# A planned two-block transformer kernel: normalizations in halves, one-pass turning of the remainder, and two head-start items moved behind the first maxima

## The chip, the cores and the metric

One Trainium2 chip, and of it one core. The core has five engines with a queue each: TensorE (PE in the profile; its weight loads are PEld), VectorE (DVE), ScalarE (ACT), GpSimd (POOL) and SyncE (SP, which here only issues DMAs). The metric is the device time of one execution in microseconds (us).

## The reference

Two transformer blocks run one after the other on x of 2 batches x 512 tokens x 144 columns, in float32, with 16 heads of 9 columns. Each block is modulated by six vectors from a condition. The second block's attention is causal, and its MLP uses SiLU where the first has GELU.

```python
ada = silu(c) @ W_ada + b_ada
shift_msa, scale_msa, gate_msa, shift_mlp, scale_mlp, gate_mlp = split(ada, 6)
h = layernorm(x) * (1 + scale_msa) + shift_msa
x = x + gate_msa * attention(h)            # softmax(q k^T / 3) v, then @ W_proj + b_proj
h = layernorm(x) * (1 + scale_mlp) + shift_mlp
x = x + gate_mlp * (gelu(h @ W_fc1 + b_fc1) @ W_fc2 + b_fc2)
# block 2: the same, causal mask, silu in the MLP, weights Wq, Wk, Wv, Wp, W1, W2
```

## The kernel before

**Tiling.** 512 tokens are 4 tiles of 128. The 144 columns are 128 columns and a remainder of 16. A normalization (l, b, k) belongs to block l, batch b, and attention (k 0) or MLP (k 1). It consists of items: `stats` (VectorE: mean and variance of each tile, L1191 to L1196; then GpSimd: `rstd`, L911), `norm` (VectorE: hn, L1204), `hr` (the remainder is modulated and split into a high and a low part in hs, five instructions, L715 to L719, on GpSimd or VectorE), and two `hT` items (TensorE turns hn or hs with four matmuls against an identity, L1350; ScalarE copies the result to hT or hT_s, L1007 and L1003). The last number of such an item is its part: 0 is all four tiles, 1 and 2 are halves. Before the change only the very last normalization runs in halves.

**Attention.** The heads are handled in 16 groups of 4: groups 0 to 3 are block 1, batch 1; 4 to 7 block 1, batch 2; 8 to 11 and 12 to 15 the same for block 2. For each group g there are 16 `max` items (TensorE: queries x keys, L1396; VectorE: the maximum of each row, L1247, or L1244 with the mask in block 2), `msplit` (GpSimd: four small instructions, L967 to L970), `mT` (TensorE turns the maxima, L1406; ScalarE copies, L1043; GpSimd sends them by DMA into rows of QS, L978), 16 `scores` items (TensorE, L1417; ScalarE: exp into probs, L1053), four `pv` items (TensorE: probs x V, four matmuls each, L1437), and `o` (ScalarE copies OT, L1060; TensorE turns it, L1444; VectorE divides, L1259 and L1260). I write M2:5 for the sixth max item of group 2 and S2:5 for the scores. `qk` makes queries and keys, `mid` and `low` split them in three bf16 parts, which go to DRAM (SP, L758) and come back as rows of QS and KS (SP, L771), `v` the values; `aT` and `proj` the output projection, `fc1`, `tanh`, `gate`, `fc2` and `fc2b` the MLP. `agate`, `acol` and GpSimd's `gated`, `fcs` and `stackw` prepare weights.

**The array.** Max and scores matmuls use half of the array's rows; two that follow each other on opposite halves run at once. pv uses quarters of its columns, everything else the whole array.

**What sets the order.** `steps` lists every item with an assumed cost, the items that it waits for, and for some a time before which it is not placed (the table `loaded`). `plan` then runs a list schedule in Python, when the program is built: on each engine it takes the item of the highest urgency (longest chain behind it, plus an offset from the table HASTE) among those that can start soon. SLACK says how soon, HOLD and OTHERS how many of the seven PSUM banks a stream may hold (three for max and three for scores). Where the plan expects TensorE to wait and its load to be low, it puts in `FILL` matmuls, identity times identity, whose result nobody reads (L1305). The plan's order is fixed in the program: on the chip each engine works strictly in that order and waits on semaphores. So a late item delays everything behind it on its engine. A program that prints the order lists what stands on each engine.

## Time and profile before

| | before |
|---|---|
| median of 3 runs | 301.45 us (299.92 to 302.79) |
| profiled execution, device time | 298.9 us |
| its span in the trace | 297.2 us |
| TensorE busy | 278.5 us, 94% |
| VectorE busy | 223.8 us, 75% |
| ScalarE busy | 185.5 us, 62% |
| GpSimd busy | 111.0 us, 37% |
| granted TensorE clock, mean | 0.994 |

The profiled execution is 2.6 us under the median of the three timed ones; 1.7 us of it lie outside the span. The page gives busy times and the costliest groups of instructions, the trace gives each instruction with its start and what ended the idle time before it. A TensorE matmul of float32 shows as two records. Durations of matmuls are modelled from issue to drained result, so neighbours overlap; how long TensorE is held is read from one start to the next.

### The profile page before, as it was taken

The numbers are of one execution on the slowest core, as the hardware profiler recorded it, in microseconds if no ns is written. First come the engines' busy times: TensorE is split into PE (matmuls) and PEld (weight loads), VectorE is DVE, ScalarE is ACT, GpSimd is POOL, SyncE is SP. The second block draws the span as 40 slices with busy tenths as digits, with TensorE's granted clock in tenths as the row PEclk, the third lists the DMA queues.
The fourth block names the chain that finished last, engine by engine and source line by source line (L and its number), as shares of the span: only waits on it lengthen the run. The fifth ranks groups of instructions, "written<-read, shape, count | busy, mean of one in ns | idle before, by whom it ended". The sixth has DMA issues, their size and how long they took to land.

```text
span 297.2 us, 5866 instructions
## 1 busy us (share of the span) xinstructions
PE 278.5 (94%) x1855; PEld 139.6 (47%) x1855; DVE 223.8 (75%) x674; ACT 185.5 (62%) x405; POOL 111.0 (37%) x242
## 2 busy tenths in 40 slices
PE   5999899999999999999998799999998999999996
PEld 4946444243243544543333434943422444344975
DVE  6859999999799986866465687498996997514761
ACT  2242326788876679667786469175756786895160
POOL 6104855936515232051331350144354455640100
PEclk9999999999999999999999999999997999999999
DMA  7514575452000000000045200000353000000001
GB/s 219 125 16 126 163 192 164 145 159 91 3 2 2 5 0 2 2 0 0 5 123 157 82 1 0 4 1 5 92 166 106 2 3 4 2 2 1 21 22 40
DMA packets 19038, 16.75 MB, mean 56 GB/s; under 512 B 2410, under 2 KB 18477, under 8 KB 19008
## 3 DMA queue, kind: packets, MB, share of 16 engines
q1 hardware_dynamic: 17214, 15.63, 18.2%
q10 hardware_dynamic: 706, 0.55, 0.6%
q0 software_dynamic: 1088, 0.20, 0.4%
q8 instruction: 15, 0.25, 0.3%
q14 instruction: 15, 0.12, 0.1%
HBM read 9.34 MB, written 6.34 MB: 53 GB/s over the span
## 4 chain that ended last, share of the span: by engine, by line
PE 68%; DVE 10%; issue 8%; ACT 8%; DMA 4%; POOL 3%; ACTq 0%; POOLq 0%
PE OB L1437 13%; PE PB L1417 9%; PE PB L1396 8%; PE PB L1471 6%; PE PB L1487 5%; ACT probs L1053 4%; PE PB L1305 4%; DVE top L1247 3%; PE PB L1444 3%; PE PB L1360 3%; PE PB L1350 2%; DMA QS<-mT 2%; PE PB L1338 2%; PE PB L1463 2%; PE PB L1472 2%
## 5 line engine op out<-in xcount | busy, mean ns | idle before, releaser
L1053 ACT ACTIVATE probs<-PB 128x512 f32<-128x512 f32 (+3 forms) x256 | 113.6, 523 | 44.6 <-PE PB L1417 32.2
L1247 DVE TENSOR_REDUCE top<-PB 128x1 f32<-128x512 f32 x128 | 79.7, 680 | 5.8 <-PE PB L1396 5.4
L1244 DVE CUSTOM_DVE_ANT_0 PB<-PB,mask_qk 128x128 f32<-128x128 f32 (+3 forms) x128 | 58.9, 521 | 10.4 <-PE PB L1396 10.3
L1396 PE MATMUL PB<-KS,QS 61*128 61x512 bf16 (+3 forms) x256 | 59.7, 345 | 2.5 <-issue 1.1
L1417 PE MATMUL PB<-QS,KS 64*128 64x512 bf16 (+3 forms) x256 | 58.0, 344 | 2.3 <-DMA QS<-mT 1.7
L1437 PE MATMUL OB<-probs,V 128*10 128x512 f32 (+3 forms) x512 | 57.0, 524 | 0.8 <-POOL probs L954 0.6
L1417 PEld LDWEIGHTS PB<-QS,KS 64*128 64x128 bf16 x256 | 16.7, 94 | 35.5 <-issue 22.1
L1396 PEld LDWEIGHTS PB<-KS,QS 61*128 61x128 bf16 x256 | 16.6, 94 | 33.9 <-issue 21.1
L954 POOL TENSOR_SCALAR_AFFINE_SELECT probs<-probs 128x512 f32<-128x512 f32 x32 | 20.3, 636 | 25.9 <-ACT probs L1053 24.9
L978 POOL DMA_DIRECT2D QS<-mT x32 | 18.5, 579 | 28.0 <-ACT mT L1043 27.1
L1305 PE MATMUL PB<-ident 128*128 128x128 f32 x116 | 23.9, 328 | 3.9 <-POOL ident L855 3.4
L1305 PEld LDWEIGHTS PB<-ident 128*128 128x128 f32 x116 | 18.1, 216 | 11.2 <-issue 5.3
L1471 PE MATMUL PB<-hT,w_fc 128*128 128x512 f32 (+3 forms) x50 | 22.0, 526 | 0.1
L911 POOL TENSOR_TENSOR rstd<-veps,half 128x4 f32<-128x4 f32 (+1 forms) x9 | 8.7, 968 | 30.2 <-DVE veps L1196 30.2
L903 POOL TENSOR_TENSOR parts<-rest,parts 108x512 bf16<-108x512 f32 x8 | 9.2, 1154 | 25.3 <-ACT parts L1025 25.3
L1437 PEld LDWEIGHTS OB<-probs,V 128*10 128x10 f32 x512 | 8.1, 89 | 20.8 <-issue 12.9
L1244 DVE DVE_READ_ACCUMULATOR2_ANT top<- 128x1 f32 x128 | 17.8, 139 | 0.0
L1268 DVE TENSOR_TENSOR X<-X,PB 128x288 f32<-128x288 f32 x16 | 7.2, 451 | 14.0 <-PE PB L1487 10.2
L1007 ACT ACTIVATE hT<-PB,mod 128x512 f32<-128x512 f32 (+1 forms) x9 | 6.7, 743 | 16.0 <-PE PB L1350 16.0
L1487 PE MATMUL PB<-g_fc,U 128*128 128x144 f32 (+1 forms) x120 | 15.7, 286 | 0.0
L1487 PEld LDWEIGHTS PB<-g_fc,U 128*128 128x128 f32 (+1 forms) x120 | 15.0, 190 | 0.9 <-ACT probs L1053 0.9
L1472 PE MATMUL PB<-hT_s,w_fc_s 96*128 96x512 f32 (+3 forms) x25 | 15.3, 612 | 0.0
(155 smaller groups left out, 404.3 us busy)
## 6 DMA issues: line engine op xcount, KB each, us to landing
qk_parts<-parts SPq DMA_DIRECT2D x16, 162.0 KB
QS<-qk_parts SPq DMA_DIRECT2D x16, 162.0 KB
KS<-qk_parts SPq DMA_DIRECT2D x16, 162.0 KB
qk_parts<-parts SPq DMA_DIRECT2D x18, 108.0 KB
qk_parts<-parts SPq DMA_DIRECT2D x16, 54.0 KB
w_fc<-in_L_cond_W_fc SPq DMA_DIRECT2D x2, 288.0 KB
w_fc<-in_L_cond_W SPq DMA_DIRECT2D x2, 288.0 KB
out<-X SPq DMA_DIRECT2D x4, 144.0 KB, 1.9
```

Of the source, the lines that this page charges most:

```text
L954: nc.gpsimd.affine_select(out=p, in_=p, compare_op=ALU.is_ge, fill=0.0, base=0, pattern=[[0, HG], [1, P]], channel_multiplier=-1).then_inc ...
L978: pool.dma_start(QS[b][STRIP * q + SROW:STRIP * (q + 1), h // 2:h // 2 + 2, :], mT[6 * q:6 * q + 6, g % 2, :]).then_inc(m_in[g % 2], 16)
L1053: nc.scalar.activation(probs[:, kt % 2, j, q0:T], bank_of(item)[:, q0:T], ACT.Exp, scale=SCALE).then_inc(bank_free[BANK[item]], 1)
L1244: ins = nc.vector.tensor_tensor_reduce(bank[:, 0:w], bank[:, 0:w], mask_qk[:, T - w:T], 1.0, NEG, ALU.add, ALU.max, m)
L1247: ins = nc.vector.tensor_reduce(m, bank[:, 0:w], AX.X, ALU.max)
L1305: nc.tensor.matmul(bank[:, 0:P], ident[:, :], ident[:, :], start=True, stop=True)
L1396: ins = nc.tensor.matmul(bank[:, 0:w], QS[b][rows, i, qt * P:(qt + 1) * P], KS[b][rows, i, 0:w], start=True, stop=True)
L1417: ins = nc.tensor.matmul(bank[:, q0:T], KS[b][rows, i, kt * P:(kt + 1) * P], QS[b][rows, i, q0:T], start=True, stop=True)
L1437: ins = nc.tensor.matmul(OB[CT * j:CT * j + VW, q0:T], V[b][:, kt, h + j, :], probs[:, kt % 2, j, q0:T], start=(kt == 0), stop=(kt == NT - 1))
L1471: nc.tensor.matmul(bank[0:w, tok], w_fc1[l][:, cols], hT[in_last(l, b)][:, tok], start=True, stop=False)
L1472: nc.tensor.matmul(bank[0:w, tok], w_fc1_s[l][:, cols], hT_s[in_last(l, b)][:, tok], start=False, stop=True).then_inc(filled_bank, 1)
L1487: ins = nc.tensor.matmul(bank[:, t * C:(t + 1) * C], (xh if in_last(l, b) else U)[0:w, c, tok], g_fc2[l][b][0:w, c, :], start=c == 0 and n ...
```

## The change

1. **Halves.** `normed_in` names the normalizations that stay whole (the first of each batch in block 1, and the MLP's of block 2, batch 1). The four others, (0,0,1), (1,0,0), (0,1,1) and (1,1,0) as block, batch, kind, now run in two halves, and the first half of each stands between the two `proj` or the two `fc2` items. qk, v and fc1 wait for both.
2. **The remainder's turning.** The matmuls of `hT` with r = 1 are float32r matmuls against a float32r identity (`identr`, one more VectorE copy at the start), no longer float32 transposes.
3. **The remainder on VectorE.** The second half's `hr` of the four moves from GpSimd to VectorE (`ON_DVE`).
4. **Times in `loaded`.** The second batch's first `stats` may be placed only from 33 us of the plan's time (before: 8), `fcs` of block 1 from 45 (33), `gated` of block 1 from 47 (40).
5. **The planner.** Streams max and scores get a bonus while they hold few banks (`FEED`), the limits of banks and SLACK change, and all of HASTE is new, so that the order changes nearly everywhere. The plan's filler matmuls are 48 (before 58).

```diff
+def normed_in(l, b, k):
+    return (0,) if (l, b, k) in ((0, 0, 0), (0, 1, 0), (L - 1, 0, 1)) else (1, 2)
+def norm_items(l, b, k, n):
+    parts = normed_in(l, b, k)
+    items = [[(kind, l, b, k, s) for kind in ("stats", "norm", "hr")] for s in parts]
+    turned = [("hT", l, b, k, r, s) for s in parts for r in range(2)]
+    if len(parts) == 1:
+        return ([], items[0], turned)[n + 1 if n < 2 else 0] if k == 0 and l == 0 else ([], [], items[0] + turned)[n]
+    return ([], items[0], items[1] + turned)[n]
...
-        return ([("aT", l, b, r, 0) for r in range(2)] + [("proj", l, b, i) for i in range(2)]
-                + [("stats", l, b, 1, 0), ("norm", l, b, 1, 0), ("hr", l, b, 1, 0), ("hT", l, b, 1, 0, 0), ("hT", l, b, 1, 1, 0)]
-                + mlp_items(l, b, 0) + [(kind, l, b, i) for i in range(2) for kind in ("fc2", "fc2b")])
+        return ([("aT", l, b, r, 0) for r in range(2)] + [("proj", l, b, 0)] + norm_items(l, b, 1, 1) + [("proj", l, b, 1)] + norm_items(l, b, 1, 2)
+                + mlp_items(l, b, 0) + [(kind, l, b, 0) for kind in ("fc2", "fc2b")] + (norm_items(l + 1, b, 0, 1) if l == 0 else [])
+                + [(kind, l, b, 1) for kind in ("fc2", "fc2b")])
...
-ON_DVE = [("hr", 0, 0, 0, 0), ("hr", 1, 1, 1, 1), ("hr", 1, 1, 1, 2)]
+ON_DVE = [("hr", 0, 0, 0, 0), ("hr", 0, 0, 1, 2), ("hr", 1, 0, 0, 2), ("hr", 0, 1, 1, 2), ("hr", 1, 1, 0, 2), ("hr", 1, 1, 1, 1), ("hr", 1, 1, 1, 2)]
...
-    loaded = {("acol", 0, 0): 5600, ("stats", 0, 0, 0, 0): 4800, ("wcopy", 0): 6000, ("stats", 0, 1, 0, 0): 8000,
+    loaded = {("acol", 0, 0): 5600, ("stats", 0, 0, 0, 0): 4800, ("wcopy", 0): 6000, ("stats", 0, 1, 0, 0): 33000,
...
-HOLD = {"attend": 3, "max": 3, "shift": 3}
-OTHERS, CALM = 2, 5
+FEED = {"max": (453000, 533000), "attend": (319000, 939000)}
+HOLD = {"attend": 3, "max": 3, "shift": 2}
+OTHERS, CALM = 3, 4
...
-    "gather": (-89000, -1231000, -28000, -333000, -1129000, -586000, -1383000, 3000, 2000, 51000, 391000, 342000, -1000, 0, 240000, 37000),
+    "gather": (-517000, -329000, -20000, -613000, -85000, -415000, -273000, -4000, 0, -126000, -181000, -165000, 311000, 44000, 189000, -75000),
...
-SLACK = {"PE": 100, "ACT": 0, "DVE": 200, "POOL": 100}
+SLACK = {"PE": 100, "ACT": 0, "DVE": 0, "POOL": 500}
...
+            dve.wait_ge(consts, 1)
+            nc.vector.tensor_copy(identr[:, :], ident[:, :])
...
-                        src = hs[:, t, :].bitcast(F32) if r else hn[:, t, 0:P]
-                        n = SR if r else P
-                        ins = nc.tensor.transpose(bank[0:n, t * P:(t + 1) * P], src, ident[:, :])
+                        o = bank[0:SR if r else P, t * P:(t + 1) * P]
+                        ins = (nc.tensor.matmul(o, hs[:, t, :], identr[:, :], start=True, stop=True) if r
+                               else nc.tensor.transpose(o, hn[:, t, 0:P], ident[:, :]))
```

The order on VectorE from the first batch's last qk split on, before. L1191 to L1204 are the second batch's first normalization, L1247 the maxima of groups 0 to 2, L1221 and L1227 the splits of the second batch's queries and keys:

```order
L1191 BN_STATS stat<-X 128x6 x4
L1194 BN_AGGR mean<-stat 128x2 x4
L1196 TENSOR_SCALAR veps<-mean 128x4
L1247 TENSOR_REDUCE top<-PB 128x1 x6
L1204 TENSOR_SCALAR hn<-X,mean,rstd 128x144 x4
L1247 TENSOR_REDUCE top<-PB 128x1 x9
L1221 TENSOR_TENSOR rest<-PB,parts 72x512
L1247 TENSOR_REDUCE top<-PB 128x1
L1227 TENSOR_TENSOR parts<-rest,parts 72x512
L1221 TENSOR_TENSOR rest<-PB,parts 108x512
L1247 TENSOR_REDUCE top<-PB 128x1 x8
```

The same place in the changed kernel, where every line number is 25 higher:

```order
L1272 TENSOR_REDUCE top<-PB 128x1 x16
L1216 BN_STATS stat<-X 128x6 x4
L1219 BN_AGGR mean<-stat 128x2 x4
L1221 TENSOR_SCALAR veps<-mean 128x4
L1229 TENSOR_SCALAR hn<-X,mean,rstd 128x144 x4
L1272 TENSOR_REDUCE top<-PB 128x1 x16
L1246 TENSOR_TENSOR rest<-PB,parts 72x512
L1272 TENSOR_REDUCE top<-PB 128x1
L1252 TENSOR_TENSOR parts<-rest,parts 72x512
L1246 TENSOR_TENSOR rest<-PB,parts 108x512
```

All 16 maxima of group 0 now come first, then the statistics, and directly behind them hn, with no maximum between.

GpSimd at the same place, before, from the second batch's rstd to the DMA of group 0's maxima (L939 to L943, L876 and L878 are `fcs`, the first MLP's weights):

```order
L911 TENSOR_TENSOR rstd<-veps,half 128x4
...
L719 TENSOR_TENSOR hs<-hy,hs 128x4x16
L939 MEMSET w_fc_s 96x576
...
L876 CAST w_fc_s<-raw_f 17x576 x2
L878 TENSOR_TENSOR w_fc_s<-raw_f,w_fc_s 17x576
L967 CAST msp<-top 128x4x2x2
...
L970 TENSOR_TENSOR msp<-mrest,msp 128x4x2x2
L903 TENSOR_TENSOR parts<-rest,parts 108x512
L978 DMA QS<-mT 3x2x512 x2
```

And in the changed kernel (here lines are 23 higher), up to the weights:

```order
L990 CAST msp<-top 128x4x2x2
L991 TENSOR_TENSOR mrest<-top,msp 128x16
L992 CAST msp<-mrest 128x4x2x2
L993 TENSOR_TENSOR msp<-mrest,msp 128x4x2x2
L934 TENSOR_TENSOR rstd<-veps,half 128x4
L1001 DMA QS<-mT 3x2x512 x2
L738 TENSOR_TENSOR hy<-hn,modr 128x64
...
L742 TENSOR_TENSOR hs<-hy,hs 128x4x16
L962 MEMSET w_fc_s 96x576
```

Group 0's maxima are split and sent ahead of the second batch's remainder and of the weights; only its rstd stands between.

On VectorE, behind the second batch's first `proj` in block 1 (L1293, before L1268), the changed kernel has this (L1269 are masked maxima of block 2, two rows each):

```order
L1293 TENSOR_TENSOR X<-X,PB 128x288
L1269 ISA PB,top<-PB,mask_qk 128x128
L1269 ISA top 128x1
L1216 BN_STATS stat<-X 128x6 x2
L1219 BN_AGGR mean<-stat 128x2 x2
L1221 TENSOR_SCALAR veps<-mean 128x2
...
L1229 TENSOR_SCALAR hn<-X,mean,rstd 128x144 x2
L1293 TENSOR_TENSOR X<-X,PB 128x288
L1269 ISA PB,top<-PB,mask_qk 128x256
L1269 ISA top 128x1
L1216 BN_STATS stat<-X 128x6 x2
```

Before, both additions to X came first, then the statistics of four tiles; now the first half's statistics and hn lie ahead of the second addition.

## Rows read from the trace of the kernel before

**Rows 1.** The page: busy time, share of the span, instructions.
```profile
PE 278.5 (94%) x1855; PEld 139.6 (47%) x1855; DVE 223.8 (75%) x674; ACT 185.5 (62%) x405; POOL 111.0 (37%) x242
```

**Rows 2.** Busy time by stretch (windows).
```profile
core 0: us, PE busy (x) PEld busy (x) DVE busy (x) ACT busy (x) POOL busy (x), PEclk, DMA share, GB/s
23.48:45.51 22.03, 20.33 (x103) 11.02 (x102) 21.32 (x44) 6.92 (x13) 12.37 (x22) 1.00 0.59 169
45.51:95.18 49.67, 49.18 (x345) 18.31 (x344) 45.65 (x92) 38.42 (x76) 25.80 (x60) 1.00 0.27 81
149.45:200.84 51.39, 46.41 (x329) 24.37 (x325) 36.64 (x138) 33.07 (x72) 14.15 (x32) 1.00 0.18 53
225.00:230.00 5.00, 4.90 (x31) 1.32 (x34) 3.63 (x21) 2.70 (x8) 2.40 (x4) 0.68 0.30 86
```

**Rows 3.** TensorE in order of time: start us, us, line, op, tiles, shapes, count.
```profile
23.48 0.60 PE L1396 MATMUL PB<-KS,QS 61*128 61x512 bf16 x3
24.01 0.49 PE L1305 MATMUL PB<-ident 128*128 128x128 f32 x2
24.43 0.39 PE L1396 MATMUL PB<-KS,QS 61*128 61x512 bf16 x1
24.75 0.49 PE L1305 MATMUL PB<-ident 128*128 128x128 f32 x2
...
94.62 0.63 PE L1444 MATMUL PB<-ident,OT 128*128 128x128 f32 x4
95.18 0.39 PE L1396 MATMUL PB<-KS,QS 61*128 61x512 bf16 x1
```

**Rows 4.** VectorE in order of time, from the second batch's statistics on.
```profile
24.81 0.69 DVE L1196 TENSOR_SCALAR veps<-mean 128x4 f32<-128x4 f32 x1
25.41 3.67 DVE L1247 TENSOR_REDUCE top<-PB 128x1 f32<-128x512 f32 x6
29.00 1.14 DVE L1204 TENSOR_SCALAR hn<-X,mean,rstd 128x144 f32<-128x144 f32 x4
...
36.20 0.68 DVE L1247 TENSOR_REDUCE top<-PB 128x1 f32<-128x512 f32 x1
```

**Rows 5.** GpSimd: a split beside L1196, and group 0's maxima.
```profile
24.32 1.15 POOL L903 TENSOR_TENSOR parts<-rest,parts 108x512 bf16<-108x512 f32 x1 [1.01 <-ACT parts L1025]
37.14 0.61 POOL L967 CAST msp<-top 128x16 bf16<-128x16 f32 x1
40.52 1.24 POOL L978 DMA_DIRECT2D QS<-mT  x2 [0.29 <-POOL parts L903]
```

**Rows 6.** TensorE: values from the remainder (float32r), then the remainder turned.
```profile
22.40 0.44 PE L1378 MATMUL PB<-w_s,hT_s 96*128 96x144 f32 x2
22.67 0.70 PE L1378 MATMUL PB<-raw,hT 128*128 128x144 f32 x4
...
32.01 0.61 PE L1350 MATMUL PB<-ident,hs 128*96 128x128 f32 x4 [0.62 <-POOL hs L719]
32.55 0.39 PE L1396 MATMUL PB<-KS,QS 61*128 61x512 bf16 x2
```

**Rows 7.** The second batch's MLP normalization in block 1, on VectorE and GpSimd.
```profile
166.55 0.45 DVE L1268 TENSOR_TENSOR X<-X,PB 128x288 f32<-128x288 f32 x1 [0.53 <-PE PB L1463]
167.10 0.94 DVE L1191 BATCH_NORM_STATS2 stat<-X 128x6 f32<-128x144 f32 x4
168.49 0.17 DVE L1196 TENSOR_SCALAR veps<-mean 128x4 f32<-128x4 f32 x1
...
168.75 1.03 POOL L911 TENSOR_TENSOR rstd<-veps,half 128x4 f32<-128x4 f32 x1 [3.94 <-DVE veps L1196]
...
172.71 0.32 POOL L715 TENSOR_TENSOR hy<-hn,modr 128x64 f32<-128x64 f32 x1
...
173.99 0.30 POOL L719 TENSOR_TENSOR hs<-hy,hs 128x64 fp32r<-128x64 f32 x1
```

**Rows 8.** What VectorE waited for over the whole span: us, times, longest (waits).
```profile
DVE hn L1204 <- POOL rstd L911: 3.4, 3, 2.4
```

More of the change, by code:

```diff
@@ L452, in plan @@
                     calm = at["PE", "max"] == 0 or at["PE", "attend"] == len(queues["PE", "attend"])
+                    if group in FEED and sum(mine) < 2:
+                        pressed = FEED[group][sum(mine)]
                     if sum(mine) >= HOLD.get(group, CALM if calm else OTHERS):
@@ L709, in remainder @@
             if earlier:
-                full(eng, ("hT", *earlier[-1], 1, 0))
+                full(eng, ("hT", *earlier[-1], 1, normed_in(*earlier[-1])[-1]))
             else:
```

62 lines of the change are left out of this document (33 added, 29 removed).

## The prediction

> **What bounds the kernel now.** I read the page first: TensorE is busy 94% of the span, VectorE 75%, ScalarE 62% [rows 1]. Shares over the whole span hide where a second engine binds, so next the windows. Between the first max matmul and M6:0 VectorE too is nearly full: 21.32 of 22.03 us, then 45.65 of 49.67 us, beside TensorE's 49.18 [rows 2]. There both are full, and neither can gain alone. From 149 to 201 us, where the second batch passes from block 1 to block 2, TensorE is busy for 46.41 of 51.39 us and VectorE for 36.64 [rows 2]: there both wait for chains. Then the order in time, for what TensorE is held by. Three max matmuls take 0.53 us (two at once, 0.22, the third 0.22, and 0.09 for the turn from half of the array's rows to all); a max followed by such a turn 0.32 us; a filler with a turn on each side 0.42 us, so 0.22 without them [rows 3]. Last, I placed a landmark: the fourth `o` starts at 94.62 us and the matmul of M6:0 at 95.18 us [rows 3].
>
> **Counting both orders.** I counted the TensorE items of both programs up to M6:0 and behind it. Most are the same in both and drop out of a difference. Counted from M0:0 (23.48 us):
>
> - Up to M6:0, before: 68 scores, 16 pv, 4 o, 94 turns, 23 fillers. Changed: 62 scores, 14 pv, 3 o, 80 turns, 14 fillers, 2 fewer pairs at once.
> - Behind M6:0, before: 187 turns, 24 fillers, 145 pairs. Changed: 227 turns, 22 fillers, 162 pairs, and the 6 scores, 2 pv and the o that were not done.
>
> **Step 1, the head, up to M6:0: -3.7 us.** In the changed kernel VectorE sets this stretch. It has 96 maxima, at 0.60 us each (six take the 3.59 us from 25.41 to 29.00 [rows 4]) 57.6 us. To that come, each read from such a row or a neighbour of it, the statistics 1.5, hn 1.1, four splits of queries and keys 2.5, three o 1.5, three agate and two acol 2.2 us. And there is a new wait. Before, six maxima lie between statistics and hn; now nothing does. GpSimd's rstd takes about 1.03 us [rows 7], so VectorE stands for 1.2 us with handovers, unless GpSimd is still at the split of group 0, which needs 1.5 us from 33.5 us on and is done as the statistics end. Sum 67.6 us. VectorE starts the maxima at 23.8 instead of 25.41 us [rows 4], since the statistics are no longer ahead of them, so it is through at 91.4 us. TensorE may be some maxima ahead of it (three banks), which allows 90 us for the matmul of M6:0. Its own work is smaller, 61.7 us by the counts, which alone would allow 85 us. As both interfere at times (before, VectorE stood for some 4 us in this stretch though it was nearly full), I take 91.5 us, against 95.18. Scores start some 5 us earlier, because GpSimd takes up group 0's maxima at about 33.6 instead of 37.14 us and sends them at about 36.8 instead of 40.52 us [rows 5]. But by itself this is worth nothing: the maxima don't run faster.
>
> GpSimd's weights that moved behind cost nothing: it is busy 25.80 of 49.67 us [rows 2], and fc1 and proj need them only after 99 us. The second batch's rows arrive later, by up to 7 us by my reading, and are due at M4:0, at about 69 us; I see about 2 us of cover. If it is gone, each us more is a us lost.
>
> On beside-work the Trainium skill has a rule that speaks against the move. L1196 took 0.69 us while GpSimd's L903 ran from 24.32 to 25.47 us [rows 4, 5], and 0.17 us with GpSimd idle [rows 7]. The page "GPSIMD Engine Reference" (Specifications) says that GpSimd's SBUF ports are shared with VectorE and collide with VectorE instructions of some kinds. By that rule the moved statistics, now beside GpSimd's four instructions on group 0's maxima, could be stretched again, by some 0.5 us; the trace agrees as far as this one row goes. By the row alone the price is 0 to 0.5 us, and it was paid before too, so the sum has nothing for it.
>
> **Step 2, TensorE's content behind M6:0: +4.4 us.** Forty turns more at 0.09 are +3.6 us. Two fillers fewer are -0.4. 17 pairs more, less 6 scores more: -1.0 us by width (block 2's are narrower, down to 128 columns). Two pv and one o that were put off are +2.5 us. The turned remainder: before, four take 0.54 us [rows 6]. A float32r matmul of 144 columns took 0.135 us [rows 6], four would be 0.54 us too, a gain of nothing; its weights have 128 columns where hs has 96, so at best three quarters, 0.40 us. I take 0.5 us less over all of them. (From the row, 0 to 1.1 us.)
> The page "TensorE: Matmul & The Clock Gate" (LDWEIGHTS) gives a weight load columns divided by 1.2 ns, 80 ns for 96 columns. By it four would be 0.32 us and the gain some 1.8 us in all, which is 1.3 us under my sum; no row here has such a load alone.
> Sum: 3.6 - 0.4 - 1.0 + 2.5 - 0.5 = 4.2, and rounding of the tally 0.2.
>
> **Step 3, halves: -4.4 us.** fc1 and qk need both halves, so what counts is the chain from the last addition to X on. It loses half of the statistics (1.32 us, L1191 and L1194: -0.65), half of hn (1.1 us [rows 4]: -0.55), and in place of GpSimd's 1.58 us from 172.71 to 174.29 us [rows 7] VectorE does half a remainder, 0.75 us (-0.8); half of the turning goes too (-0.2). That is 2.2 us. rstd stays: 1.03 us [rows 7] is nearly all fixed cost. Four normalizations are halved, but only where TensorE waits does it count. (0,0,1) and (1,0,0) run while it is full. (0,1,1) and (1,1,0) lie in the stretch with 5 us of idle time [rows 2] and most of the late fillers. 2 x 2.2 = 4.4 us, less than the idle time there. Bounds: 0, if other waits take its place, and -8, if fillers go with it.
>
> **Step 4, not changed.** The order from the last `o` on, some 26 us, is the same but for line numbers. The clock's dip (0.68 of full speed in 5 us, 1.6 us lost [rows 2]) may come or not; I leave it.
>
> **Sum.** Span 297.2 - 3.7 + 4.4 - 4.4 = 293.5 us. 1.7 us outside it: 295.2 against 298.9 us of the profiled execution. That one was 2.6 us under the median of the timed runs, 301.45 us, and I predict their median: **297.8 us**, 1.2% faster.
>
> **The rivals.**
> *A. The halves give nothing (chance 0.31).* TensorE's waits at the second batch's passage are then for the exp chain and the maxima's DMA, not for the norms; the new order has as many fillers there as before (16 against 17), which speaks for it. Then step 3 is 0 to -2: 300 to 302 us, no difference to be told from none. That the halves don't shorten the chain at all, as each needs its own rstd, comes to the same.
> *B. Each half makes VectorE stand for its rstd (0.24), slower.* Now VectorE stood three times, 3.4 us in all, for rstd [rows 8]. In halves there are four waits more, and at (1,0,0) the new order puts hn directly behind the statistics. GpSimd works in order too, and a wait of its own (a causal cut, a DMA that waits for ScalarE) then holds VectorE. At 1.2 us each, with the head's, it is 6 us on VectorE. It decides the time when VectorE's waits for rstd pass some 5 us and fall where the maxima are needed next; with nothing from step 3, the time is 302.2 + 3 = 305 us. Against it: three of the first halves have one to four maxima between.
> *C. TensorE's content alone decides (0.12, of the 0.45 for faster).* If VectorE's idle time in the head is not needed, M6:0 comes at 90 us, and fillers shrink the passage: 293.5 to 295 us.
>
> **How the numbers follow.** My case, 296 to 298.4 us, has 0.33 and is the likeliest, C 0.12, A 0.31, B 0.24. Under 1% nothing can be told from no change by this kernel's measurement; a part of my case's upper end falls there, and a part of A's under it, which cancel. Faster by over 1% (under 298.4 us) 0.45, within 1% 0.31, slower (over 304.5 us) 0.24. The range holds 8 in 10: 292.5 to 305.5 us, from C's lower end to B's price. My own case's range is 294.5 to 301.
>
> **What would show it.** Step 1: M6:0 near 91.5 us, VectorE with one idle time of about 1.2 us before L1229 at 35 us and full otherwise; wrong if M6:0 is later than 94 us, or if TensorE waits at M4:0 for rows of QS and KS. Step 2: the span from M6:0 to the end no shorter than before if step 3 fails. Step 3: from the second proj's addition to the first fc1 matmul at (0,1,1) about 2 us shorter, and TensorE's idle time in the passage down to 1 us or less. Wrong in all: the waits for rstd over 6 us, or another clock dip.

## The result: slower by 3.8%, and the profile after

| | before | changed |
|---|---|---|
| median | 302.12 us (299.92 to 303.82) | 312.87 us (311.59 to 316.12) |
| ratio | | 1.0376, 95% interval 1.027 to 1.0482 |
| span of the profiled execution | 297.2 us | 309.6 us |
| granted TensorE clock, mean | 0.994 | 0.967 |

I had predicted 297.8 us (292.5 to 305.5). The direction was wrong, and the time lies outside the range. Medians are over all timed executions of a kernel; a ratio leaves out those that ran over 1.5% slower than its fastest, so the two can differ a little.

The page's busy times of the changed kernel, to be held against [rows 1]:

```profile
PE 284.2 (92%) x1835; PEld 139.0 (45%) x1835; DVE 229.1 (74%) x699; ACT 187.5 (61%) x413; POOL 112.4 (36%) x246
```

TensorE is busy 5.7 us longer with 20 records fewer, and the span grew by 12.4 us. So part is work and part is standing; a part of the longer work is the same matmuls at a lower clock, as shown below. The starts of `o` (the turning of a group's output) are landmarks that both programs pass. TensorE's rows at o1 and o7, before and then changed:

```profile
72.47 0.52 PE L1444 MATMUL PB<-ident,OT 128*128 128x128 f32 x3
161.03 0.63 PE L1444 MATMUL PB<-ident,OT 128*128 128x128 f32 x4 [0.81 <-ACT OT L1060]
```
```profile
78.67 0.55 PE L1471 MATMUL PB<-ident,OT 128*128 128x128 f32 x3
170.90 0.66 PE L1471 MATMUL PB<-ident,OT 128*128 128x128 f32 x4
```

Four stretches: up to o1 +6.2 us (and one `agate` is still to do), o1 to o7 92.2 instead of 88.6 us (+3.7), o7 to o9 54.5 instead of 51.7 us (+2.8), from o9 to the end 84.2 instead of 84.5 us (-0.3). Together 12.4 us; by the ratio of the timed executions it is 11.4. This table of `o` starts (us) holds every run, and the experiments below are read by it. M0:0 is the start of the first max matmul, and the clock is the granted clock, as a share of full speed, from o7 to o9:

| kernel | M0:0 | o1 | o7 | o9 | end | o1-o7 | o7-o9 | clock there | o9-end |
|---|---|---|---|---|---|---|---|---|---|
| before | 23.5 | 72.5 | 161.0 | 212.7 | 297.2 | 88.6 | 51.7 | 1.00 | 84.5 |
| b1_onepass_only | 24.7 | 73.8 | 162.3 | 215.3 | 300.0 | 88.5 | 53.0 | 0.97 | 84.7 |
| g1_weights_only | 24.3 | 74.1 | 162.7 | 216.7 | 301.7 | 88.6 | 54.0 | 0.97 | 85.0 |
| g2_onepass_loads_later | 24.0 | 75.5 | 164.0 | 219.7 | 303.0 | 88.5 | 55.7 | 0.94 | 83.3 |
| f2_fillers_in_whole | 24.5 | 73.7 | 167.5 | 218.4 | 303.1 | 93.8 | 50.9 | 1.00 | 84.7 |
| f3_fillers_in_half | 24.3 | 73.3 | 171.4 | 223.8 | 309.3 | 98.1 | 52.4 | 0.97 | 85.5 |
| changed | 23.6 | 78.7 | 170.9 | 225.4 | 309.6 | 92.2 | 54.5 | 0.94 | 84.2 |
| c1_fill_head | 24.0 | 78.1 | 170.3 | 226.9 | 311.4 | 92.2 | 56.6 | 0.91 | 84.5 |
| c2_fill_both | 24.2 | 78.9 | 171.1 | 225.7 | 311.1 | 92.2 | 54.6 | 1.00 | 85.4 |
| c3_transposes_back | 24.6 | 79.5 | 171.8 | 228.0 | 312.5 | 92.3 | 56.2 | 0.91 | 84.5 |
| c4_loads_later | 23.2 | 77.1 | 169.3 | 225.5 | 310.1 | 92.2 | 56.2 | 0.91 | 84.6 |
| d1_head_before | 24.6 | 85.4 | 177.7 | 232.3 | 316.7 | 92.2 | 54.7 | 0.97 | 84.4 |
| d2_norm_early | 24.1 | 84.4 | 176.6 | 233.0 | 317.7 | 92.2 | 56.4 | 0.91 | 84.7 |
| d3_whole_norms | 24.1 | 81.2 | 178.6 | 241.9 | 326.6 | 97.4 | 63.3 | 0.89 | 84.8 |
| e3_whole_on_vector | 24.0 | 79.3 | 173.7 | 230.6 | 316.4 | 94.4 | 56.9 | 0.97 | 85.8 |
| g3_norm_early | 24.6 | 80.9 | 173.1 | 226.3 | 311.2 | 92.2 | 53.2 | 1.00 | 84.9 |
| f4_scores_later | 24.5 | 81.5 | 173.7 | 227.3 | 313.0 | 92.2 | 53.6 | 0.97 | 85.7 |
| e1_before_then_after | 24.2 | 79.5 | 171.8 | 224.7 | 309.4 | 92.3 | 52.9 | 1.00 | 84.7 |
| e2_after_then_before | 25.3 | 83.4 | 173.9 | 226.3 | 309.4 | 90.5 | 52.4 | 1.00 | 83.1 |
| f1_head_to_o1 | 24.0 | 75.2 | 168.4 | 223.4 | 307.6 | 93.2 | 55.0 | 0.97 | 84.2 |

The column o1-o7 repeats to 0.1 us in all kernels that have the same order there. Two other stretches don't. From M0:0 to o1, five kernels with the changed head untouched (changed, c3, d3, e3, f4) take 54.9 to 57.1 us, and M0:0 itself starts between 23.2 and 25.3 us: a difference of 1 us at o1 says little. And o7-o9 follows the granted clock. In the changed order it is 52.9 and 53.2 us at a clock of 1.00, 54.5 at 0.94 and 56.2 to 56.6 at 0.91; in the order before, 50.9 and 51.7 us at 1.00, 53.0 and 54.0 at 0.97 and 55.7 at 0.94. (It isn't exact: f3 and f1, at 0.97, took 52.4 and 55.0.) The window of the changed kernel, then of e1:

```profile
170.90:225.40 54.50, 48.65 (x307) 24.92 (x306) 39.69 (x147) 31.02 (x71) 18.00 (x37) 0.94 0.08 24
```
```profile
171.80:224.70 52.90, 46.68 (x307) 24.65 (x306) 39.54 (x147) 30.85 (x72) 18.03 (x37) 1.00 0.08 24
```

So of the +2.8 us there, about 1.3 are the order (53.0 less 51.7), and about 1.5 go with the dip of the clock. In that 1.5 is a longer stand of TensorE for the rows of S8:0, 1.8 us against 1.4 in e1 and 1.1 in g3.

**The head.** TensorE of the changed kernel in order of time, and behind it VectorE and GpSimd's sending of group 0's maxima:

```profile
34.99 0.39 PE L1433 MATMUL PB<-identb,msp 128*12 128x128 bf16 x4 [2.82 <-POOL msp L993]
35.31 1.62 PE L1330 MATMUL PB<-ident 128*128 128x128 f32 x6
37.63 1.03 PE L1423 MATMUL PB<-KS,QS 61*128 61x512 bf16 x3 [0.70 <-DMA KS<-qk_parts]
38.60 1.11 PE L1376 MATMUL PB<-ident,hn 128*128 128x128 f32 x4
39.64 1.03 PE L1423 MATMUL PB<-KS,QS 61*128 61x512 bf16 x3
43.22 1.01 PE L1444 MATMUL PB<-QS,KS 64*128 64x512 bf16 x3 [2.54 <-DMA QS<-mT]
```
```profile
36.29 1.16 DVE L1229 TENSOR_SCALAR hn<-X,mean,rstd 128x144 f32<-128x144 f32 x4 [1.19 <-POOL rstd L934]
38.28 3.89 DVE L1272 TENSOR_REDUCE top<-PB 128x1 f32<-128x512 f32 x6 [0.83 <-PE PB L1423]
44.69 2.48 DVE L1272 TENSOR_REDUCE top<-PB 128x1 f32<-128x512 f32 x4 [2.52 <-PE PB L1423]
```
```profile
36.71 1.22 POOL L1001 DMA_DIRECT2D QS<-mT  x2 [0.46 <-POOL rstd L934]
```

VectorE did get through group 0's maxima earlier, and the maxima were sent at 36.71 us, as predicted. But then TensorE stands three times: for the split maxima (2.82 us), for the rows of group 1 (0.70) and at S0:0 for the maxima it is to use (2.54), which land only at 43.2 us, 6.5 us after the first of their two issues began. Each issue took 4.5 to 5.7 us to land; the same two in the kernel before, from 40.5 us on, took 2.9 and 3.1. Everything behind these items on TensorE stands too, the maxima M1:6 and on among them, so VectorE starves for 0.83 and 2.52 us. The kernel before at the same places:

```profile
37.70 0.60 PE L1396 MATMUL PB<-KS,QS 61*128 61x512 bf16 x3
...
45.50 0.39 PE L1396 MATMUL PB<-KS,QS 61*128 61x512 bf16 x1
45.51 0.60 PE L1417 MATMUL PB<-QS,KS 64*128 64x512 bf16 x2
```

M1:0 started at 37.70 us before and at 37.63 us now. The head start is gone there, as group 1's rows don't land earlier. Until then the old order had the second batch's turning and its three `qk` to do; and S0:0 came at 45.5 us behind twelve maxima of group 1, with no wait. The same in windows, changed and then before:

```profile
33.50:50.00 16.50, 11.76 (x47) 4.97 (x47) 11.43 (x29) 5.85 (x11) 9.39 (x19) 0.59 0.58 156
```
```profile
33.50:50.00 16.50, 16.02 (x82) 8.47 (x85) 15.22 (x29) 7.39 (x15) 9.32 (x16) 1.00 0.65 180
```

VectorE (third busy time) does 11.43 instead of 15.22 us in 16.5, at a granted clock of 0.59 (mostly 0.50, the 1.2 GHz level), after TensorE had stood. From M0:0 to M6:0 VectorE is busy as long as before (66.5 against 67.0 us); its idle time grew from 4.7 to 8.8 us.

### The profile page after: what moved, and what is told of

The parts are those of the page before. It is cut to its first block, busy times and chain, and to the rows that moved or that the text cites. A ratio compares the mean times of both kernels' runs of the same rounds, so it can differ in the third digit from the quotient of the medians.

```text
span 309.6 us, 5896 instructions
## 1 busy us (share of the span) xinstructions
PE 284.2 (92%) x1835; PEld 139.0 (45%) x1835; DVE 229.1 (74%) x699; ACT 187.5 (61%) x413; POOL 112.4 (36%) x246
## 4 chain that ended last, share of the span: by engine, by line
PE 67%; DVE 13%; DMA 6%; ACT 5%; issue 5%; POOL 4%; ACTq 0%; POOLq 0%; DVEq 0%
PE OB L1464 14%; PE PB L1444 10%; PE PB L1423 9%; PE PB L1515 5%; PE PB L1499 5%; DMA QS<-mT 4%; DVE top L1272 4%; PE PB L1387 3%; ACT probs L1076 3%; PE PB L1490 2%; PE PB L1363 2%; PE PB L1471 2%; PE PB L1405 2%; DVE stat L1216 2%; POOL rstd L934 1%
## 5 line engine op out<-in xcount | busy, mean ns | idle before, releaser
L1076 ACT ACTIVATE probs<-PB 128x512 f32<-128x512 f32 (+3 forms) x256 | 114.9, 522 | 43.4 <-PE PB L1444 24.2
L1444 PE MATMUL PB<-QS,KS 64*128 64x512 bf16 (+3 forms) x256 | 62.7, 359 | 6.1 <-DMA QS<-mT 4.7
L1269 DVE CUSTOM_DVE_ANT_0 PB<-PB,mask_qk 128x128 f32<-128x128 f32 (+3 forms) x128 | 59.1, 518 | 9.1 <-PE PB L1423 8.8
L1423 PE MATMUL PB<-KS,QS 61*128 61x512 bf16 (+3 forms) x256 | 63.1, 362 | 1.3 <-DMA KS<-qk_parts 0.7
L1444 PEld LDWEIGHTS PB<-QS,KS 64*128 64x128 bf16 x256 | 17.1, 94 | 42.3 <-issue 25.7
L1423 PEld LDWEIGHTS PB<-KS,QS 61*128 61x128 bf16 x256 | 16.8, 94 | 38.8 <-issue 17.9
L1330 PE MATMUL PB<-ident 128*128 128x128 f32 x96 | 19.9, 338 | 3.4 <-POOL ident L878 3.4
L934 POOL TENSOR_TENSOR rstd<-veps,half 128x2 f32<-128x2 f32 (+1 forms) x13 | 10.3, 789 | 27.8 <-DVE veps L1221 27.7
L990 POOL CAST msp<-top 128x16 bf16<-128x16 f32 x16 | 4.0, 247 | 44.9 <-issue 18.3
L1030 ACT ACTIVATE hT<-PB,mod 128x256 f32<-128x256 f32 (+1 forms) x13 | 8.1, 621 | 18.3 <-PE PB L1376 18.3
L1066 ACT ACTIVATE mT<-PB 12x512 bf16<-12x512 bf16 x16 | 9.2, 578 | 16.1 <-PE PB L1433 16.1
L1330 PEld LDWEIGHTS PB<-ident 128*128 128x128 f32 x96 | 15.5, 229 | 7.6 <-issue 3.7
L1293 DVE TENSOR_TENSOR X<-X,PB 128x288 f32<-128x288 f32 x16 | 7.2, 450 | 14.9 <-PE PB L1515 7.5
L1269 DVE DVE_READ_ACCUMULATOR2_ANT top<- 128x1 f32 x128 | 17.9, 140 | 0.0
L1515 PE MATMUL PB<-g_fc,U 128*128 128x144 f32 (+1 forms) x120 | 17.0, 291 | 0.0
```

The lines of the kernel that those rows point to most:

```text
L934: nc.gpsimd.tensor_tensor(rstd[:, t0:t1], veps[:, t0:t1], half[:, t0:t1], ALU.pow).then_inc(rstd_ready, 1)
L1076: nc.scalar.activation(probs[:, kt % 2, j, q0:T], bank_of(item)[:, q0:T], ACT.Exp, scale=SCALE).then_inc(bank_free[BANK[item]], 1)
L1269: ins = nc.vector.tensor_tensor_reduce(bank[:, 0:w], bank[:, 0:w], mask_qk[:, T - w:T], 1.0, NEG, ALU.add, ALU.max, m)
L1330: nc.tensor.matmul(bank[:, 0:P], ident[:, :], ident[:, :], start=True, stop=True)
L1423: ins = nc.tensor.matmul(bank[:, 0:w], QS[b][rows, i, qt * P:(qt + 1) * P], KS[b][rows, i, 0:w], start=True, stop=True)
L1444: ins = nc.tensor.matmul(bank[:, q0:T], KS[b][rows, i, kt * P:(kt + 1) * P], QS[b][rows, i, q0:T], start=True, stop=True)
```

## The experiments

Each time is a median; the ratio, with its 95% interval, is to the kernel before on the same chip. A ratio within 2% of 1 counts as no difference.

**1. Is it the clock?** Fillers ahead of the three items of the head that wait, then at the passage too.

```diff
+FILL.update({("mT", 0): 12, ("max", 1, 0): 6, ("scores", 0, 0): 14})
```
```diff
+FILL.update({("proj", 0, 1, 0): 3, ("scores", 8, 0): 8, ("scores", 8, 3): 2, ("hT", 0, 1, 1, 0, 1): 2})
```

> The changed kernel with the same order on every engine and 28 filler matmuls more, in three places where TensorE stood idle in the head: 12 instead of 1 ahead of the turning of group 0's maxima (idle 2.8 us there), 6 instead of 3 ahead of M1:0, 14 instead of 0 ahead of S0:0 (idle 2.5 us, for a DMA). Theory A, the clock: the profile after shows 1.2 GHz granted from 34.8 to 48.8 us, right behind these idle times; with TensorE busy there the grant stays at 2.4 GHz, the first `o` comes 3 to 4 us earlier (62 us instead of 65.5) and the time falls by 3 to 5 us. Theory B, waits for data: TensorE waited for GpSimd and DMAs, the clock cost nothing that wasn't waited for anyway; the time stays within 1 us. Theory C, the order's content and VectorE: the same, no change.

> As the run before, and 15 fillers more in the second batch's passage: 3 ahead of its first proj, 8 ahead of S8:0 (idle 1.8 us), 2 ahead of S8:3 and 2 ahead of its first hT. The profile after shows the granted clock at 1.2 GHz from about 179 to 185 us. Theory A: this is worth 2 to 3 us more than the head's fillers alone. Theories B and C: nothing, or a loss of up to 1 us by fillers in the way.

Measured: 314.01 us, ratio 1.0438 (1.0337 to 1.0539), and 313.59 us, 1.0442 (1.032 to 1.0565). The clock was kept; the window of the head in the first run, and of o7 to o9 in the second:

```profile
33.50:50.00 16.50, 14.51 (x97) 8.67 (x95) 12.33 (x29) 5.96 (x12) 9.41 (x19) 1.00 0.59 160
```
```profile
171.10:225.70 54.60, 50.01 (x338) 28.06 (x337) 39.62 (x147) 30.98 (x72) 18.57 (x37) 1.00 0.08 23
```

o1 came 0.6 us earlier (1.0 from M0:0 on), not several, as S0:0 still started at 43.27 us when its rows landed. In the head the low clock was mostly a symptom of standing. For the passage these fillers settle less: they held the clock, but there are 15 of them, each work of its own, and the stretch took 54.6 us where e1 and g3, at a clock of 1.00 without them, took 52.9 and 53.2. So these fillers cost about what they gave, and the 1.5 us that go with the dip stay in the account.

**2. The one-pass turning, taken out of the changed kernel (c3, shown), then put alone into the one before (b1, the other way round).**

```diff
-                        ins = (nc.tensor.matmul(o, hs[:, t, :], identr[:, :], start=True, stop=True) if r
-                               else nc.tensor.transpose(o, hn[:, t, 0:P], ident[:, :]))
+                        ins = nc.tensor.transpose(o, hs[:, t, :].bitcast(F32) if r else hn[:, t, 0:P], ident[:, :])
```

> The changed kernel in the same order, but the remainder is turned by float32 transposes again, as before the change. The prediction had 0.5 us for it (0 to 1.1). In the profile after, two such float32r matmuls take 0.29 to 0.36 us, four in the head at half clock 0.73 us against 0.84 us before. So 0 to 1 us slower. A theory in which the new form itself harms (its load of the weights, or how it counts for the clock) would show 1 us or more faster, with the clock higher.

> The kernel before with one part of the change alone: the remainder is turned by one-pass float32r matmuls. Order and all else as before. By my term (0.5 us over all of them) 301.6 us, nothing that can be told; by the rule on weight loads 1.8 us less, 300.3 us. A changed kernel with the old turning was 1.8 us slower, which points the same way as the second, but its intervals overlap.

Measured: 314.63 us, 1.0473 (1.0367 to 1.058), and 301.66 us, 0.9929 (0.9871 to 0.9987). It is no part of the loss. The second is the only kernel here with an interval under 1, though it reaches from 0.4 to 3.9 us of gain, and stays within 2%. Its rows show what a set of four turnings holds TensorE, 0.45 us from start to start against 0.54 [rows 6]:

```profile
33.19 0.53 PE L1352 MATMUL PB<-identr,hs 128*96 128x128 f32 x4 [0.61 <-POOL hs L720]
33.64 0.39 PE L1399 MATMUL PB<-KS,QS 61*128 61x512 bf16 x2
```

Eight such sets (32 matmuls in the trace) are 0.7 us, near my term of 0.5. The page "TensorE: Matmul & The Clock Gate" of the Trainium skill (LDWEIGHTS) gives a weight load as columns divided by 1.2 ns; worked out for 96 columns that is an estimate of 80 ns, or 0.32 us for four turnings. The row says 0.45, so this trace doesn't agree. The gain by the ratio, 2.1 us, is nearer to the estimate's 1.8 than to my 0.5, but this measurement can't separate them, and experiment 3 has a kernel with the same turnings and no gain.

**3. Do the rows land late because the queues are full?** SyncE issues the second block's weights only when group 0's maxima have landed.

```diff
 if (l, b, i) == (0, 0, NC - 1):
+    sp.wait_ge(m_in[0], 32)
     load_second_qkv()
```

> The changed kernel with one wait more, on SyncE: the loads of later weights, which went out from 37.0 us on, beside group 0's maxima, wait until those have landed. The maxima's DMA took 5.7 us to land, where 1.8 us is the median. Theory B: S0:0 comes at about 41 instead of 43.2 us and the time falls by 1 to 3 us, the clock's stretch at 1.2 GHz being shorter too. Theory A: it helps only by what it shortens of that stretch, 1 us at most. If the rows of QS and KS, which went out from 30.6 us on, are what holds the DMA, nothing changes.

> The kernel before with one-pass turnings, and SyncE waits for group 0's maxima before it loads the second block's weights, so that the rows of queries and keys do not share the queues with them. In the changed kernel that brought o1 1.6 us earlier, as TensorE stood there for rows. In this order TensorE does not wait for rows in the head, so nothing is expected from it: 299 to 302 us, as with the one-pass turnings alone; under 299 us if the queues' load matters here too.

Measured: 311.46 us, 1.0368 (1.027 to 1.0467). In the head it did what was asked, in part:

```profile
41.99 1.00 PE L1445 MATMUL PB<-QS,KS 64*128 64x512 bf16 x3 [2.13 <-DMA QS<-mT]
```

S0:0 started at 41.99 instead of 43.22 us, and o1 came 1.6 us earlier (77.1). Of both, 0.4 us is that this execution's M0:0 was earlier; TensorE still stood 2.13 us for the maxima, which took 4.2 to 4.9 us to land. That agrees with the reading that landings set the head, but 1.2 us is less than the head's own scatter. The passage then was 1.7 us longer, at a clock of 0.91 instead of 0.94. In the kernel before, with one-pass turnings, 304.46 us, 1.0033 (0.9984 to 1.0081): no gain. TensorE doesn't stand for rows there, so none was due; but against the one-pass turnings alone (0.9929) it is 1% slower. Either the wait costs that, or the 0.7% of experiment 2 was chance.

**4. The head's order, spliced.** On every engine the old order up to a cut, the changed order behind it (or the other way round in e2). HEAD lists the items of the first part.

```diff
+ORDER = {e: HEAD[e] + [i for i in ORDER[e] if i not in HEAD[e]] for e in ORDER}
```

> The changed kernel with the head's order of before: on every engine the items that stood ahead of the first agate come in the order of before (second batch's statistics, hn, turning and qk splits between the maxima of groups 0 and 1), all else in the changed order; only the weights stay behind. Theory 1 (the head lost its cover: rows of KS for group 1 land at about 37.6 us in either kernel, and before had the second batch's turning and qk, about 4.5 us of TensorE's work, to do until then): M6:0 back at about 95 us instead of 99.3, and the time 4 to 5 us under the changed kernel's 312.9, so about 308 to 309 us. Rival 2 (the head's loss only shifts work, and what is behind M6:0 sets the end): time within 1 us of the changed kernel, 312 to 314 us.

> The head is now cut at the first o, where both orders have done nearly the same items (the changed one 3 maxima and 3 scores more), so that the seam starves nobody: before's order up to the first o on every engine, the changed order behind it. Theory 1 (the head is the loss of the changed kernel up to M6:0, as the second batch's turning and qk no longer fill the wait for rows): the first o at about 59.5 to 60.5 us instead of 65.5, M6:0 at about 95, time 307 to 309 us, half way back to before. Rival 2 (VectorE or the rest takes the gain back): over 311 us.

> The mirror: the changed kernel's order up to the first o, before's order (whole normalizations, turnings as before) behind it. Theory 1: the first o at 65.5 us, and the time 302.1 + 4 to 6 less 1 for the six items done earlier: 305 to 307 us. Rival 2: under 303.5 us. If this and its mirror add up to both kernels' distance (10.8 us), head and rest are independent terms, and the rest of the changed order alone costs 5 to 6 us, with its halves.

> Before's order on every engine up to the second o, the changed order behind it; there both have done the same items but for two maxima (and one agate more in before), so the seam has no stall of its own. If the head is the main loss: o1 at 72.5 to 74 us (changed kernel 78.7), o1 to o7 92.2 less 1.5 for the agate, o7 to o9 53 to 54.5, the rest 84.2: the time 302.5 to 306 us. If the rest takes the gain back (VectorE or a later wait sets the pace), 309 to 312 us.

Measured: 317.91 us, 1.0473 (1.0356 to 1.059); 310.99 us, 1.0371 (1.0331 to 1.0411); 312.06 us, 1.0387 (1.0334 to 1.044); 310.13 us, 1.0307 (1.0235 to 1.038). The first is a failed experiment: at its cut the rest began with eight scores in a row, TensorE stood for exps, and VectorE starved for 10.4 us between 44 and 74 us. The second and third cut at o0, but o0 to o1 still took 17.1 and 16.0 us instead of 13.1. So they don't give the head's price. What e2 does show is that the changed head makes o0 late on the old code too (67.4 against 59.4 us; from M0:0, 42.1 against 35.9): the order does it, not the halves or the one-pass turning. The last cut, at o1, where both orders have done the same items but two maxima, is fair:

```profile
75.17 0.63 PE L1491 MATMUL PB<-ident,OT 128*128 128x128 f32 x4
168.36 0.66 PE L1491 MATMUL PB<-ident,OT 128*128 128x128 f32 x4
```

o1 is 3.5 us earlier than in the changed kernel, the span 2.0 us shorter. I had expected 302.5 to 306 us. Putting the head's order right gave back only 2.0 of the 12.4 us: o1 was still 2.7 us later than in the kernel before, and o1 to o7 took 93.2 us, though with one `agate` less in it I had counted on 90.7. At that seam VectorE was full (13.70 of 14.30 us from o1 to o2). So this spliced order paid at its seam too, and 2.0 us is a lower bound of the head's price.

**5. Which move in the head?** Normalization back (first with the banks as they were, then with banks given out anew), and the weights alone moved in the kernel before.

The turnings go behind M0:8 and M0:11, the statistics behind the last qk split of the first batch, hn behind M0:5; `fcs` goes behind the sending of group 0's maxima.

```diff
+MOVED = {"PE": [(("hT", 0, 1, 0, 0, 0), ("max", 0, 8)), (("hT", 0, 1, 0, 1, 0), ("max", 0, 11))],
+         "DVE": [(("stats", 0, 1, 0, 0), ("qk", 0, 0, 2)), (("norm", 0, 1, 0, 0), ("max", 0, 5))],
...
```
```diff
+at = ORDER["POOL"].index(("mT", 0)) + 1
+ORDER["POOL"][at:at] = [("fcs", 0, 0), ("fcs", 0, 1)]
```

> The changed kernel with only the second batch's first normalization (statistics, hn, remainder, the two turnings) back between the maxima of group 0; its qk splits stay behind the maxima of group 1. Theory 1: VectorE still cannot begin group 1 before about 37.6 us, and the qk work still comes after; only the turning (about 1.2 us at half clock) and hn leave the stretch behind 37.6 us: 310.5 to 312.5 us. If VectorE's stand of 1.2 us for rstd and the statistics' place were what cost the head its time, 308 to 309 us, as in the run with the whole head.

> The changed kernel with the second batch's first normalization (statistics, hn, remainder, its two turnings) back at before's places between the maxima of group 0, and banks given out anew up to group 2, so that no turning waits for a bank (which was what made the run with the early normalization slow: the first mT at 42.5 us). The qk splits stay behind group 1. If the normalization's place cost the head its time: o1 at 74 to 75.5 us instead of 78.7, the time 309 to 311 us. If it was the qk work that no longer fills the wait for group 1's rows: o1 at 77.5 to 79 us, the time 311.5 to 313.5 us.

> The kernel before with one move alone: GpSimd's weights of the first MLP (fcs) behind the sending of group 0's maxima. By my step 1 it is worth nothing either way: o1 at 72.5 to 73.8 us, the time 301 to 303 us. If GpSimd's place mattered for the head, group 0's maxima would be sent earlier than 40.5 us and o1 come earlier than 72 us.

Measured: 318.38 us, 1.0539 (1.0458 to 1.062); 315.75 us, 1.0479 (1.0406 to 1.0551); 302.69 us, 0.9998 (0.9938 to 1.0058). The first failed by itself, as a turning stood for a bank that a maximum held. In the second no turning stood for a bank, and o1 was at 80.9 us, 2.2 later (1.2 from M0:0 on) and not 4 earlier: the normalization's place by itself gives nothing back. Its longest stand, and VectorE's waits up to 76 us:

```profile
45.57 1.01 PE L1457 MATMUL PB<-QS,KS 64*128 64x512 bf16 x3 [3.44 <-DMA QS<-mT]
```
```profile
DVE top L1285 <- PE PB L1436: 7.5, 7, 4.1
```

The maxima are sent later (40.55 us), S0:0 still stands behind six maxima of group 1, and VectorE behind both. The weights cost and give nothing, as predicted. What is left in the head, by elimination, is TensorE's order behind M1:5: the scores ahead of M1:6 and on, and `qk` behind group 1. No run moved either of them alone, so this is argued and not shown.

**6. What does a turn cost?** 24 fillers more between o1 and o7 of the kernel before, once where no turn is added, once where each adds two.

The first entries of each list:

```diff
+FILL.update({("aT", 0, 0, 0, 0): 2, ("aT", 0, 0, 1, 0): 2, ("proj", 0, 0, 1): 2, ("fc1", 0, 0, 0, 0): 2,
...
```
```diff
+FILL.update({("scores", 2, 7): 1, ("scores", 2, 12): 1, ("max", 4, 7): 1, ("scores", 3, 0): 1, ("max", 4, 12): 1,
...
```

> The kernel before with 24 fillers more between o1 and o7, each ahead of a whole-array item that follows a whole-array item: work without a turn. By 0.22 us a filler, o1 to o7 grows from 88.5 to at most 93.8 us; less where TensorE had idle time there (2.5 us of it).

> The kernel before with 24 fillers more between o1 and o7, each between two half-array items: the same work and 48 turns more. If a turn costs 0.09 us, o1 to o7 is 4.3 us longer than in the run with the fillers at whole-array items. If turns cost nothing when VectorE or ScalarE sets the pace: no longer than that run.

Measured: 306.14 us, 1.0193 (1.01 to 1.0287), and 308.23 us, 1.0259 (1.0165 to 1.0353). o1 and o7 of each:

```profile
73.73 0.52 PE L1445 MATMUL PB<-ident,OT 128*128 128x128 f32 x3
167.53 0.63 PE L1445 MATMUL PB<-ident,OT 128*128 128x128 f32 x4 [0.81 <-ACT OT L1061]
```
```profile
73.29 0.63 PE L1445 MATMUL PB<-ident,OT 128*128 128x128 f32 x4
171.40 0.63 PE L1445 MATMUL PB<-ident,OT 128*128 128x128 f32 x4 [0.81 <-ACT OT L1061]
```

93.8 and 98.1 us, against 88.6: 5.2 us for 24 fillers (0.22 each) and 4.3 us more for 48 turns (0.09 each). Both came out as expected to 0.1 us. The changed order has 27 turns more between o1 and o7 (2.4 us) and the `agate` that it does later (1.6 to 1.8 us); with two maxima less (0.4) that makes the measured 3.7 us. My count of turns takes in changes to and from pv; the fillers priced only those between half the rows and the whole array, which are 24 of the 27.

**7. Halves and the passage.** The four normalizations whole again, with the remainder on GpSimd and then on VectorE; and `proj(0,1,1)` with two maxima ahead of S8:0.

`whole` drops the items of part 1 and makes part 2 the whole.

```diff
+ORDER = {e: whole(items) for e, items in ORDER.items()}
+ON_DVE = [("hr", 0, 0, 0, 0)] + [("hr", *part, 0) for part in WHOLE] + [("hr", 1, 1, 1, 1), ("hr", 1, 1, 1, 2)]
```
```diff
+at = ORDER["PE"].index(("max", 9, 0))
+ORDER["PE"][at:at + 10] = [('max', 9, 0), ('max', 9, 1), ('proj', 0, 1, 1), ('max', 9, 2), ('max', 9, 3), ('scores', 8, 0), ('scores', 8, 1), ('scores', 8, 2), ('scores', 8, 3), ('scores', 8, 4)]
```

> The changed kernel's order with the four halved normalizations whole again (each at the place of its second half, the remainder on GpSimd). If the halves give nothing, as rival A said: 312 to 314 us. If they give the 2.2 us each that I priced at two places: 316 to 317.5 us. If their own waits and handovers cost time (rival B): 309 to 311 us, and the chain from the second batch's first proj to the first fc1 (15 us now) gets shorter.

> The changed kernel with the four normalizations whole again, but the remainder left on VectorE, at the second half's place (the run with whole normalizations and the remainder on GpSimd had 6.7 us of waits of pv for GpSimd's causal cuts, which queued behind the remainder). If that queue was all of its 14.8 us, this one comes at 312 to 314 us and the halves alone are worth nothing. If halves are worth what I priced (2.2 us at each of two places), 316 to 318 us. Over 320 us: the halves are worth more than priced in this order, since its items behind them stand ready for the earlier time.

> The changed kernel with one edit of TensorE's order at the passage: proj(0,1,1) and M9:2 and M9:3 ahead of S8:0, which stood 1.79 us for its rows, instead of behind it. If that wait is on the path: o7 to o9 shorter by 1.5 to 2 us, the time 311 us. If the passage is held by the chain over hT and fc1 alone, also about 1 us shorter, as proj(0,1,1) comes earlier. No change within 0.5 us if the exps behind S8 set it.

Measured: 327.65 us beside 303.21 for before; 319.38 us, 1.0668 (1.0594 to 1.0742); 314.01 us, 1.0441 (1.0345 to 1.0536). In this order the halves are worth more than I had priced: without them it loses a further 2.8% (1.0668 over 1.0376), some 9 us by the ratios and 6.8 by the spans; o1 to o7 is 2.2, o7 to o9 2.4 and the rest 1.6 us longer; and with the remainder back on GpSimd, whose causal cuts queue behind it (pv stood 6.7 us for them), more still. Rival A's premise, that halves give nothing, doesn't hold here. But the order was planned for halves, and no run planned one anew without them. The third run brought the second addition to 2.95 us behind the first, where it had been 5.85, yet the first fc1 came only 0.9 us earlier behind o7 (17.0 instead of 17.9).

The passage in the changed kernel, VectorE, then GpSimd's rstd, then TensorE:

```profile
175.40 0.45 DVE L1293 TENSOR_TENSOR X<-X,PB 128x288 f32<-128x288 f32 x1 [3.21 <-PE PB L1490]
...
179.90 0.30 DVE L1269 CUSTOM_DVE_ANT_0 PB<-PB,mask_qk 128x128 f32<-128x128 f32 x1 [2.66 <-PE PB L1423]
...
180.37 0.96 DVE L1229 TENSOR_SCALAR hn<-X,mean,rstd 128x144 f32<-128x144 f32 x2
181.25 0.44 DVE L1293 TENSOR_TENSOR X<-X,PB 128x288 f32<-128x288 f32 x1
```
```profile
177.07 0.71 POOL L934 TENSOR_TENSOR rstd<-veps,half 128x2 f32<-128x2 f32 x1 [3.95 <-DVE veps L1221]
180.60 0.65 POOL L977 TENSOR_SCALAR_AFFINE_SELECT probs<-probs 128x512 f32<-128x512 f32 x1 [2.81 <-ACT probs L1076]
```
```profile
177.32 0.59 PE L1444 MATMUL PB<-QS,KS 64*128 64x512 bf16 x3 [1.79 <-DMA QS<-mT]
177.84 0.76 PE L1490 MATMUL PB<-g_proj,aT 128*128 128x144 f32 x4
...
188.83 1.12 PE L1499 MATMUL PB<-hT,w_fc 128*128 128x512 f32 x2
```

And before, the first addition and the first fc1:

```profile
165.57 0.45 DVE L1268 TENSOR_TENSOR X<-X,PB 128x288 f32<-128x288 f32 x1 [0.29 <-PE PB L1463]
```
```profile
176.06 1.10 PE L1471 MATMUL PB<-hT,w_fc 128*128 128x512 f32 x2
```

The first half's rstd is ready at 177.8 us, but its hn starts at 180.37: two masked maxima stand ahead of it on VectorE, and they wait 2.66 us for TensorE, which stands at S8:0 for its rows and then has the second `proj` to do. So the second addition comes 5.85 us after the first; before it was 0.98 us (166.55 [rows 7] less 165.57). The whole stretch from the first addition to fc1 is at a granted clock of 0.75 here, and at 1.00 in the kernel before.

## Why the prediction was wrong, step by step

M6:0 starts in the changed kernel together with M5:15 in the first of these rows of TensorE, at about 98.8 us, against 95.18 [rows 3].

```profile
98.76 0.39 PE L1423 MATMUL PB<-KS,QS 61*128 61x512 bf16 x2
98.98 0.38 PE L1444 MATMUL PB<-QS,KS 64*128 64x512 bf16 x2
```

| step | predicted | measured |
|---|---|---|
| 1, head to M6:0 | -3.7 | +3.6 |
| 2, content behind M6:0 | +4.4 | +6.3 from M6:0 to o7, where 34 of the 40 more turns lie; TensorE is busy for 69.5 of 72.1 us there |
| 3, halves | -4.4 | from o7 to the end +2.5, where step 2's tally is about -2; some 1.5 of it goes with the clock, so about +3 |
| 4, tail and clock | 0 | from o9 on -0.3; the clock about +1.5 in the passage and at most +1 in the head, within the rows above |

**Step 1 failed, and it is the sentence "VectorE sets this stretch".** The terms of VectorE's work were right (66.5 us busy, against my 66.4 and 1.2 of standing), and so was the wait of 1.2 us for rstd (1.19). What failed is that I let VectorE's work follow without a gap. Two waits that were hidden before now stood in the open: for group 1's rows, whose landing at 37.6 us the change didn't move, and for group 0's maxima, which were sent 3.8 us earlier but took 4.5 to 5.7 us to land instead of 3. VectorE's 4.0 us more of idle time are M6:0's 3.6 us of delay, where I had it 3.7 us early. I had looked for rows at M4:0 and not at M1:0 and S0:0. I read a work sum as a schedule, while my own window said that both engines were full and had no room for a stop of either. I also wrote that an earlier start of the scores is "worth nothing". By the rows it cost: an item that TensorE reaches before its data is a stop for the maxima behind it.

**Step 2 was right in mechanism and, up to o7, in size.** Turns are 0.09 us (experiment 6). M6:0 to o7 grew by 6.3 us, and my prices give 6.4 for that stretch: 34 turns 3.1, the two pv and the o put off 2.5, six scores 1.3, one filler 0.2, less 0.7 for three pairs more. Behind o7 the tally can't be told from step 3.

**Step 3 failed in its passage.** The chain that I counted did shrink, from the last addition to the first fc1 from 9.5 us (166.55 to 176.06) to 7.6 (181.25 to 188.83), and to 6.8 in e1 and g3 at full clock, against 2.2 us predicted. (Two terms in it were off: a rstd of two tiles took 0.71 us, not nearly the 1.03 of four, and the half remainder on VectorE 1.3 us, from 185.97 to 187.30, not 0.75.) But I measured it from the last addition and took that as fixed. The order put the second `proj` and the first half's hn behind an item that waits for a DMA: from the first addition to fc1 it is 13.4 us instead of 10.5, and 11.8 and 12.1 in e1 and g3 at full clock. A half's lead is spent if what stands between its statistics and its hn can wait. So the shorter chain is real, and from the first addition on it was lost again: about 1.4 us by the order, and 1.5 with the dip of the clock, which I had left out. That the second `proj` behind S8:0 is what costs the order's part is not shown: f4 moved it ahead, and fc1 gained 0.9 us at most.

**Rival B named the right side for the wrong cause.** VectorE waited 4.2 us, six times, for rstd in all, where [rows 8] had 3.4. The weights' move cost nothing, as said. The clock dipped where TensorE stood; holding it up with fillers bought 0.6 us at o1.

**What stays open.** The share of the scores' early place against that of the late `qk` in the head; why group 0's maxima took longer to land; what in the passage's order costs its 1.3 us; and why the clock dips there in some executions and not in others of one order. Head and rest are not additive terms either: taking back the head's order brought o1 forward by 3.5 us and the end by 2.0.

The lowest ratio of all is that of the kernel before with the one-pass turnings alone: 0.7% under before (0.1 to 1.3%), and by the two ratios some 4% under the changed kernel. The first is too small to call a gain, as g2 with the same turnings didn't show it; the second is the loss of the changed order.

## What to carry to other kernels

Where each engine works strictly in a planned order, don't add up work per engine only: for every item that the new order brings forward, look up when its data lands (rows of a DMA, not issue), and what stands behind it on its engine. In the head here, where two engines were both full, a stop of one became a stop of both and was not made up later. A landmark table over all runs costs nothing, and shows at once which stretches repeat to 0.1 us and can be used to price a thing. Put the granted clock beside each stretch: what looks like scatter of one order may be the clock.
